# Cross-attention and an FP4 feed-forward layer on one core: P times V as 77-row products over the whole array

## The reference

```
q = heads(layernorm(x) @ Wq.T + bq)      # 16 heads of 32 columns
k = heads(ctx @ Wk.T + bk);  v = heads(ctx @ Wv.T + bv)    # 77 keys
scores = where(mask, q @ k.T / sqrt(32), -1e9)
x = x + concat(softmax(scores) @ v) @ Wo.T + bo

fp4(t): per 16 elements scale = max(|t|)/6, values rounded to the grid 0, 0.5, 1, 1.5, 2, 3, 4, 6
gate = fp4(ln(x)) @ fp4(w_gate).T;  up = fp4(ln(x)) @ fp4(w_up).T       # 1408 wide
x = x + fp4(silu(gate) * up) @ fp4(w_down).T
```

## Time and profile before

| | |
|---|---|
| median of 3 runs | 2116.81 us |
| profiled execution | 2116.27 us |
| its span, first to last instruction | 2114.5 us |
| PE busy | 1947.6 us (92%) |
| DVE busy | 1770.4 us (84%) |
| ACT busy | 1202.3 us (57%) |
| POOL busy | 446.4 us (21%) |
| mean granted TensorE clock | 0.957 |

### The profile page before, as it was taken

One profiled execution on the slowest core, in us unless ns is written; L12 is line 12 of the kernel. 1 busy time (PEld: TensorE's weight loads), 2 busy tenths in 40 slices (PEclk: granted clock), 3 DMA queues, 4 the chain that ended last, 5 costly groups with the idle time before them and its releaser, 6 DMA issues.

```text
span 2114.5 us, 56741 instructions
## 1 busy us (share of the span) xinstructions
PE 1947.6 (92%) x21888; PEld 1217.2 (58%) x21888; DVE 1770.4 (84%) x2676; ACT 1202.3 (57%) x2487; POOL 446.4 (21%) x525
## 2 busy tenths in 40 slices
PE   6323799999999999999999999999999999999987
PEld 4222566566666666666666666666666666566543
DVE  7677688888888888888888888888888888888773
ACT  5354655666556665556665566655666655666421
POOL 5434211122111221112221112211122211222110
PEclk9655899999999999999999999999999999999998
DMA  5234376556665556656566655566565665555632
GB/s 165 77 87 90 70 138 127 129 128 136 142 139 125 133 128 146 138 126 131 129 143 142 130 125 132 131 147 134 124 137 128 143 141 126 130 127 131 128 74 56
DMA packets 726026, 265.00 MB, mean 125 GB/s; under 512 B 677879, under 2 KB 678903, under 8 KB 725983
## 3 DMA queue, kind: packets, MB, share of 16 engines
q1 hardware_dynamic: 724398, 264.43, 57.0%
q10 hardware_dynamic: 1584, 0.01, 0.1%
HBM read 65.97 MB, written 34.82 MB: 48 GB/s over the span
## 4 chain that ended last, share of the span: by engine, by line
PE 86%; issue 5%; POOL 4%; DMA 2%; DVE 1%; ACT 1%; SPq 0%; POOLq 0%; another core or an unknown queue 0%; ACTq 0%; DVEq 0%
PE psum L611 43%; PE psum L540 37%; PE psum L627 4%; POOL h_room L480 2%; PE psum L660 2%; POOL h_room L484 1%; DMA t_room<-halves 1%; DMA ph_room<-h_room 1%; PE psum L649 1%; DMA q_room<-in_L_xattn_Wk_dram 0%; SPq L355 0%; PE psum L553 0%; ACT probs L790 0%; DVE h_room L874 0%; POOL ln_rstd L507 0%
## 5 line engine op out<-in xcount | busy, mean ns | idle before, releaser
L611 PE MATMUL psum<-wguT,t_room 128*128 128x352 bf16 x6144 | 942.9, 314 | 16.6 <-DMA t_room<-halves 10.8
L611 PEld LDWEIGHTS psum<-wguT,t_room 128*128 128x128 bf16 x6144 | 597.5, 98 | 347.1 <-DMA t_room<-halves 12.4
L540 PE MATMUL psum<-wdT,ph_room 128*128 128x512 bf16 x2112 | 471.3, 382 | 12.6 <-DMA ph_room<-h_room 12.6
L540 PEld LDWEIGHTS psum<-wdT,ph_room 128*128 128x128 bf16 x2112 | 207.7, 98 | 266.0 <-DMA ph_room<-h_room 13.8
L505 POOL TENSOR_TENSOR ln_var_eps<-ln_mean_var,eps 128x1 f32<-128x1 f32 x128 | 104.3, 814 | 1214.7 <-DVE ln_mean_var L1032 1012.7
L784 ACT ACTIVATE silu_g<-psum 128x352 f32<-128x352 f32 x256 | 117.9, 460 | 425.9 <-PE psum L611 425.9
L790 ACT ACTIVATE probs<-psum,neg_max 128x77 f32<-128x77 f32 x1024 | 245.5, 350 | 4.0 <-DVE neg_max L1070 3.2
L807 ACT ACTIVATE t_room<-psum,bq_col 128x128 bf16<-128x128 f32 x256 | 73.2, 369 | 254.2 <-PE psum L540 254.2
L1064 DVE TENSOR_TENSOR h_room<-silu_g,psum 128x352 f32<-128x352 f32 x256 | 132.2, 516 | 79.6 <-ACT silu_g L784 79.6
L540 PE MATMUL psum<-t_room,wqT 128*128 128x128 bf16 x3072 | 188.6, 223 | 0.0
L540 PEld LDWEIGHTS psum<-t_room,wqT 128*128 128x128 bf16 x3072 | 178.0, 100 | 2.2
(11 more groups left out here) (103 smaller groups left out, 2576.0 us busy)
## 6 DMA issues: line engine op xcount, KB each, us to landing
io_room<-in_x_dram SPq DMA_DIRECT2D x128, 256.0 KB, 2.9
x_scratch<-x_new SPq DMA_DIRECT2D x64, 256.0 KB, 2.0
x_cur<-x_scratch SPq DMA_DIRECT2D x64, 256.0 KB, 3.4
out_dram<-io_room SPq DMA_DIRECT2D x64, 256.0 KB, 2.4
t_room<-halves SPq DMA_TRANSPOSE x192, 3.2
raw<-in_L_ffn_w_down_dram SPq DMA_DIRECT2D x4, 704.0 KB, 4.3
raw<-in_L_ffn_w_gate_dram SPq DMA_DIRECT2D x11, 256.0 KB, 2.6
raw<-in_L_ffn_w_up_dram SPq DMA_DIRECT2D x11, 256.0 KB, 2.9
```

What stands on the lines that cost most here:

```text
L540: ins = pe.matmul(dst, left(i), right(j), start=first and n == 0, stop=last and n == len(PRODUCTS) - 1)
L611: ins = pe.matmul(ps[:, 0:CW], xqT[:, i, kc, :], wguT[:, which, j, kc, cols], start=(kc == 0 and i == j), stop=(kc == KC - 1 and i == LO))
```

## The change

The keys are no longer split. The probabilities are laid out with 77 of 128 columns per head, and the same two DMA transposes put the 77 keys of each head on partitions 0 to 76. V has its keys on partitions 0 to 76 too, loaded by one DMA. P·V then is one product of 77 rows for each head and each of the three pairs of halves. On PE the first half of the queries moves ahead of the hook "norm".

```diff
--- before.py
+++ after.py
@@ -73,12 +73,9 @@
     GH = P // DK
     GROUPS = HEADS // GH
     GW = GH * KEYS
-    HALF_ROWS = P // 2
-    KJ = -(-KEYS // HALF_ROWS)
-    KN = -(-KEYS // KJ)
-    KW = KJ * KN
     VW = DK + 1
-    V_LOADS = 16 * KJ * GH
+    V_LOADS = 16
+    PAIR = HEADS // 2
     TILES = BATCH * SEQ // P
     TPB = SEQ // P
     CHUNKS = 4
@@ -115,7 +112,6 @@
         pv_ps = psum[:, 2:6, 0:GROUPS * VW].rearrange("p r (g w) -> p r g w", g=GROUPS)
         down_ps = bank[6]
         q_bank = o_bank = bank[7]
-        half_rows = [slice(h * HALF_ROWS, (h + 1) * HALF_ROWS) for h in range(2)]
         quarter = [slice(r * DK, (r + 1) * DK) for r in range(GH)]
 
 
@@ -125,7 +121,7 @@
         wdT = sb("wdT", [P, 2, IC, D], BF16)
 
         k_cur = sb("k_cur", [P, 2, GROUPS, KEYS], BF16)
-        v_cur = sb("v_cur", [P, 2, GROUPS, GH // 2, KJ, VW + 1], BF16)
+        v_cur = sb("v_cur", [P, 2, HEADS, VW + 1], BF16)
         ident = sb("ident", [P, P])
         ident_b = sb("ident_b", [P, P], BF16)
         ones_b = sb("ones_b", [3 * QUAD, P], BF16)
@@ -146,11 +142,11 @@
         zeros_b = sb("zeros_b", [P, P], BF16)
         neg_max = sb("neg_max", [P, HEADS])
         inv_sum = sb("inv_sum", [P, HEADS])
-        probs = sb("probs", [P, HEADS, KW])
-        p_h = sb("p_h", [P, 2, 2, KJ, HEADS // 2 * HALF_ROWS], BF16)
-        ph_room = sb("ph_room", [P, 2 * (HEADS // 2 * KJ + IC) * P], BF16)
-        pT = ph_room[:, 0:HEADS * KJ * P].rearrange("p (a s j g u t) -> p a s j g u t", a=2, s=2, j=KJ, g=GROUPS // 2, u=GH // 2)
-        hT_room = ph_room[:, HEADS * KJ * P:]
+        probs = sb("probs", [P, HEADS, KEYS])
+        p_h = sb("p_h", [P, 2, 2, PAIR * P], BF16)
+        ph_room = sb("ph_room", [P, 2 * (HEADS + IC) * P], BF16)
+        pT = ph_room[:, 0:2 * HEADS * P].rearrange("p (a s h t) -> p a s h t", a=2, s=2, h=PAIR)
+        hT_room = ph_room[:, 2 * HEADS * P:]
         hT = hT_room.rearrange("p (s k t) -> p s k t", s=2, k=IC)
         x1_new = sb("x1_new", [P, D])
         x1_cur = sb("x1_cur", [P, D])
@@ -301,13 +297,8 @@
 
             def load_values(b):
 
-                for j in range(KJ):
-                    keys = slice(j * KN, min((j + 1) * KN, KEYS))
-                    for r in range(GH):
-                        row = r % 2 * HALF_ROWS
-                        sp.dma_start(v_cur[row:row + keys.stop - keys.start, :, :, r // 2, j, 0:DK].rearrange("p s g d -> p (s g) d"),
-                                     v_scratch[bass.ds(b, 1), keys].rearrange("a k (n r d) -> (a k) n r d", r=GH, d=DK)[:, :, r])\
-                            .then_inc(v_loaded, 16)
+                sp.dma_start(v_cur[0:KEYS, :, :, 0:DK].rearrange("p s h d -> p (s h) d"),
+                             v_scratch[bass.ds(b, 1)].rearrange("a k (n d) -> (a k) n d", d=DK)).then_inc(v_loaded, 16)
 
             down_rows(0)
             sp.dma_start(attn_raw[0], wk.rearrange("(n p) k -> p n k", p=P)).then_inc(wk_loaded, 16)
@@ -360,8 +351,8 @@
                 def probabilities(pair):
                     after(p_lo[pair], n + 1)
                     after(pv_done, GH * n)
-                    transposed(pT[:, pair].rearrange("p s j g u t -> p (s j g u) t"),
-                               p_h[:, pair].rearrange("p s j w -> p (s j w)"), pT_loaded[pair])
+                    transposed(pT[:, pair].rearrange("p s h t -> p (s h) t"),
+                               p_h[:, pair].rearrange("p s w -> p (s w)"), pT_loaded[pair])
 
                 if values is not None:
                     after(pv_done, GH * n)
@@ -451,11 +442,11 @@
             own = Steps(pool, pool_step)
             own.did(pool.memset(ident[:], 0.0))
             own.did(pool.memset(zeros_b[:], 0.0))
-            own.did(pool.memset(v_cur[:].rearrange("p s g u j w -> p (s g u j w)").bitcast(U32), 0))
+            own.did(pool.memset(v_cur[:].rearrange("p s h w -> p (s h w)").bitcast(U32), 0))
             own.did(pool.memset(probs[:], 0.0))
-            own.did(pool.memset(p_h[:].rearrange("p a s j w -> p (a s j w)").bitcast(U32), 0))
+            own.did(pool.memset(p_h[:].rearrange("p a s w -> p (a s w)").bitcast(U32), 0))
             own.after()
-            own.did(pool.memset(v_cur[:, HI, :, :, :, DK], 1.0))
+            own.did(pool.memset(v_cur[:, HI, :, DK], 1.0))
             own.did(pool.memset(ones_b[:], 1.0))
             own.did(pool.memset(minus_half[:], -0.5))
             own.did(pool.memset(eps[:], LN_EPS))
@@ -619,16 +610,14 @@
                     if d is not None:
                         pe.wait_ge(h_done, d * CHUNKS + 3)
                     for g in range(GROUPS):
-                        for j in range(KJ):
-                            for s, t in PRODUCTS:
-                                for r, ps in enumerate(head_ps):
-
-                                    rows = half_rows[r % 2]
-                                    ins = pe.matmul(ps[:, g * VW:(g + 1) * VW], pT[rows, g // 2, s, j, g % 2, r // 2, :],
-                                                    v_cur[rows, t, g, r // 2, j, 0:VW],
-                                                    start=j == 0 and s == t, stop=j == KJ - 1 and s == LO)
-                                    if g == GROUPS - 1 and j == KJ - 1 and s == LO:
-                                        ins.then_inc(pv_done, 1)
+                        for s, t in PRODUCTS:
+                            for r, ps in enumerate(head_ps):
+
+                                head = g * GH + r
+                                ins = pe.matmul(ps[:, g * VW:(g + 1) * VW], pT[0:KEYS, head // PAIR, s, head % PAIR, :],
+                                                v_cur[0:KEYS, t, head, 0:VW], start=s == t, stop=s == LO)
+                                if g == GROUPS - 1 and s == LO:
+                                    ins.then_inc(pv_done, 1)
 
                 def queries(groups):
                     if groups.start == 0:
@@ -664,9 +653,10 @@
 
                 if b is not None:
                     weighted_values()
+                if n is not None:
+                    queries(range(GROUPS // 2))
                 weave("norm")
                 if n is not None:
-                    queries(range(GROUPS // 2))
                     queries(range(GROUPS // 2, GROUPS))
                     clear_scores()
                 if f is not None:
@@ -794,8 +784,8 @@
                 def probabilities_high(pair):
                     act.wait_ge(exp_done, 3 * n + pair + 2)
                     at_least(act, pT_loaded[pair], 16 * n)
-                    act.copy(p_h[:, pair, HI].rearrange("p j (h k) -> p h j k", k=HALF_ROWS)[:, :, :, 0:KN],
-                             probs[:, 2 * pair * GH:2 * (pair + 1) * GH, :].rearrange("p h (j k) -> p h j k", k=KN))\
+                    act.copy(p_h[:, pair, HI].rearrange("p (h k) -> p h k", k=P)[:, :, 0:KEYS],
+                             probs[:, pair * PAIR:(pair + 1) * PAIR, :])\
                        .then_inc(p_hi[pair], 1)
 
                 weave("norm")
@@ -1073,9 +1063,9 @@
 
                 def probabilities_low(pair):
                     dve.wait_ge(p_hi[pair], n + 1)
-                    high, whole = (p_h[:, pair, HI].rearrange("p j (h k) -> p h j k", k=HALF_ROWS)[:, :, :, 0:KN],
-                                   probs[:, 2 * pair * GH:2 * (pair + 1) * GH, :].rearrange("p h (j k) -> p h j k", k=KN))
-                    low(p_h[:, pair, LO].rearrange("p j (h k) -> p h j k", k=HALF_ROWS)[:, :, :, 0:KN], whole, high,
+                    high, whole = (p_h[:, pair, HI].rearrange("p (h k) -> p h k", k=P)[:, :, 0:KEYS],
+                                   probs[:, pair * PAIR:(pair + 1) * PAIR, :])
+                    low(p_h[:, pair, LO].rearrange("p (h k) -> p h k", k=P)[:, :, 0:KEYS], whole, high,
                         p_lo[pair], n + 1)
 
                 def residual():
```

## The result

The changed kernel took 2094.97 us (median of 4 runs, 2093.04 to 2099.68), before 2116.62. The ratio is 0.9903, 95% interval 0.9884 to 0.9922, that is 20.5 us less (16.5 to 24.6). Forecast were 2102 us and 14.9 us less, range 2090 to 2115: the direction and the wide range held, the gain was short by about 6 us, and the forecast's own range of 2097 to 2107 us was missed by 2 us.

The account below looks back on a forecast made before the run. PE was taken to bound the loop, the order of work the lead-in. Loop 10.6 us plus lead-in 4.3 us gave 14.9 us off 2116.27, with 0.5 for the median 2101.9, forecast 2102 us; range 2090 to 2115.

Parts of the forecast that it names:

- A new product costs 25.2 ns, so halving the count gains nothing: P·V: 48 full-height products at 25.2 ns take 1.21 us, the same as 96 at 12.6 ns.
- The rival in which loads no longer hide: P·V: short products cannot cover full-height loads, 45 ns each, about 2157 us, at the bound about 2187; chance 10%.
- the Trainium skill's rule that I weighed against the row: P·V: weight loads overlap running matmuls only in another row group, so each full-height product pays load and product in turn.
- The fast rival: P·V: the floor belongs to changing halves, so 16.3 ns per product, 0.78 us per tile, 2078 us; chance 7%.
- 0.19 us per pass from the changes of form, 10.6 us in the loop: P·V's entry and exit: without height changes 1.40 us becomes 1.21 per tile, over 56 passes.
- 77 rows count as full height: P·V beside 128-row products: no change of form; the rival that 77 rows differ gave 2112.5 us, chance 6%.
- Nobody takes it away: Loop: gate/up chunk 0's wait for xqT keeps 0.8 of 1.0 us slack, so 56 of 64 P·V gain.
- Queries ahead of the transposes, 4.3 us: Lead-in: 24 of 48 query products go before weight transposes in three passes, gaining 0.9, 2.5 and 0.9 us.
- Gain 2.5 us: Lead-in, pass 2: of 5.31 us for the queries behind the transposes, 2.6 remain, less 0.1.
- the 0.9 us of pass 3: Lead-in, pass 3: gain of 0.9 us, taking the order of pass 2 and the clock of pass 1.
- V's load 0: SP's queue at batch changes: one DMA for eight gains nothing, as PE waited for nothing behind it; bounds 0 to +3 us.
- The sum: Whole kernel: 10.6 us from the loop plus 4.3 us from the lead-in, 14.9 us less, forecast 2102 us.

Follow-up runs that it names:

- half-height run: Changed kernel with its 48 P·V products put on rows 64 to 127 alone, keys 0 to 63 left out: 2105.63 us, ratio 0.9949.
- the order alone: Kernel before with only the first half of the queries moved ahead of the hook "norm": 2108.63 us, ratio 0.9962.
- P·V alone: Changed kernel with all queries put back behind the hook "norm": 2102.93 us, ratio 0.994.

## Why the prediction was right, and where it was short

- *A new product costs 25.2 ns, so halving the count gains nothing.* Right, and shown from three sides: 48 products in 1.21 us, 96 in 2.42, and the floor between 16 and 50 columns. The inference from the 64-row form (12.6 ns, two halves) to one part of the array was sound. The rival in which loads no longer hide is refuted, and with it the Trainium skill's rule that I weighed against the row ("TensorE: Matmul & The Clock Gate", Part 3): both full height and a single half keep 25 ns with a load for each product. The fast rival is refuted by the same rows: nothing changes halves any more, and the spacing is 25 ns, not 16. The floor near 25 ns, which the same page of the Trainium skill states in Part 1, agrees with the 25.0 to 25.6 ns of 33, 16 and 50 columns. It holds for one part of the array: between its two halves the kernel before had starts 3 to 4 ns apart.
- *0.19 us per pass from the changes of form, 10.6 us in the loop.* Right: 0.20 us per pass, 10.4 to 10.9 us over 55 passes. The half-height run isolates it. That 77 rows count as full height was right: the first of them starts 0.15 us after the last gate/up product.
- *Nobody takes it away.* Right: the chunk that waits for xqT has no wait in the middle of the loop, and waits at its ends as before. One pass more waits at the start (0.27 us for the fifth tile, none before), and the 0.20 us of the fourth from the end is gone; both are small. After, the pass of the earlier trace rows's first row idles 1.44 us there in place of 1.26:

```profile
300.79 1.52 PE L602 MATMUL psum<-wguT,t_room 128*128 128x352 bf16 x9 [1.44 <-DMA t_room<-halves]
```

- *Queries ahead of the transposes, 4.3 us.* The mechanism was right, the size was not: 7.5 to 7.7 us (8.8 in the order alone). By passes, from clearing to clearing of the score banks: pass 1 gave 1.1 us with 0.3 still to be paid back (forecast 0.9), pass 2 3.9 (forecast 2.5), pass 3 2.5 (forecast 0.9). I priced the 24 queries left behind the transposes at the low clock's 2.6 us in each pass. That held in pass 1 (2.77 us). In passes 2 and 3 they ran at the high level (granted clock 1.00 in both): 1.50 us for 24. In before, P·V, transposes and queries had pauses between them; after, P·V, the first queries and the transposes follow each other from 122.61 on almost without one (PE is busy for 5.28 of the 5.52 us to 128.13), and the granted clock was 0.50 from 123.97 to 126.48, 0.80 from there to 128.13 and 1.00 behind. That the order does it is shown by its two runs: the order alone gives 1.50 us, P·V alone leaves the queries at 5.33. That it does so by closing the pauses is argued. The faster transposes gave another 0.4 us. The step that failed is "Gain 2.5 us" of pass 2, and with it the 0.9 us of pass 3, where the clock was taken from before although the order that sets it was being changed. (The sum written there, 5.31 − 2.6 − 0.1, is 2.6 and not 2.5; that is small beside the 3.9 measured.) Why the order alone gave 1.1 to 1.3 us more in the lead-in than the whole change is open; about 1.0 us of it lies behind pass 3, where nothing was reordered.
- *V's load 0.* Right: its issue fell to 1 us and, put back to 7.63 us, changed nothing. A bound of +3 us was too careful.
- *The sum.* Loop and lead-in give 18 us by the traces, the runs say 20.5 (16.5 to 24.6). The remaining 2 us are not explained; they lie inside the interval, and the prologue and the tail, which follow the clock of the single execution, are wide enough to hold them. That the result still fell in the range, although the lead-in gave 7.5 us where 4.3 was added, is owed to the width of the range.

## What to carry to other kernels

Take the price of a product from the spacing of starts in a run, per part of the array, and ask first whether the product is at a floor: 16, 33 and 50 columns cost the same here, so joining two products that share their stationary operand (0.29 us a pass) was worth more than the change of height (0.20). A short run in another height than its neighbours costs about 0.09 us at each end on top of its products, so a low-height form must save more than that. Where PE waits in a pipeline's start, move independent work ahead of the awaited item, and price it at both levels of the clock.

## What the runs showed of the hardware

- Products with a fresh load each: 25 ns at 16, 33 and 50 columns, 30.7 at 66 (77 rows over the whole array). At 33 columns it is 25 ns for 64 rows in one half too. Where 64-row products alternate between the halves, as before, two start 3 to 4 ns apart and the next two 22 ns later, 25 ns for the pair.
- A change between full height and 64 rows costs about 0.09 us each way (245 in place of 149 ns between starts on entering, 106 in place of 25 on leaving).
- SP's issue of V's load was priced by the DMA and hardly by its pieces: 2464 pieces of 64 bytes took 0.99 us in one DMA and 7.63 us in eight.
- The granted clock differed between executions of one kernel: 0.91 and 1.00 from 30 to 50 us, where the prologues differ by 1.5 us (before) and 1.8 us (after), and 0.92 and 0.96 in the tail of the changed kernel, which differs by 4.0 us.
